# Attention kernel: the loop over heads written out on all engines, and the inverse scales turned beside the third chunk of the first maxima

## The reference, cut to what matters

```python
def reference(x, ctx_2048, ...):          # x (16, 56, 256), ctx (16, 1500, 256)
    x = x + _L0_xattn_ref(_layernorm(x), ctx_2048, Wq, bq, Wkv, bkv, Wp, bp)
    x = x + _L0_ffn_ref(...)              # 32 experts of 96, top 6, and a shared one
    x = x + _L1_xattn_ref(...)            # decayed scan over the context, layernorm
    x = x + _L1_ffn_ref(...)              # 8 experts of 176, top 2
    return x

def _L0_xattn_ref(x, cond, ...):          # 16 heads of 16; 896 queries, 24000 keys, all with all
    q = _fq_sym(q * scale, axis=-1)       # rounded to 127 steps of its own maximum
    k = _fq_sym(k, axis=-1)
    v = _fq_sym(v, axis=2)
    attn = jax.nn.softmax(jnp.einsum('bhqd,bhkd->bhqk', q, k), axis=-1)
    attn = _fq_unsigned(attn, axis=-1)    # rounded to 255 steps of the row's maximum
    out = jnp.einsum('bhqk,bhkd->bhqd', attn, v)
    return out.reshape(B, N, C) @ Wp + bp
```

## Time and profile before

| | us |
|---|---|
| median of 3 runs | 5237.91 |
| runs | 5232.74 to 5238.2 |
| the profiled execution | 5235.59 |
| its span, first to last instruction | 5234.4 |
| busy: PE, DVE, ACT, POOL | 4791.3, 4165.5, 3839.6, 3616.9 |

### The profile page before, as it was taken

The page is one execution under the profiler, slowest core; times in us unless marked ns, Lnnn a source line. Parts: engine busy times, 40 slices in busy tenths (PEclk is TensorE's granted clock), DMA queues, the critical chain, the costliest instruction groups (busy, mean ns, idle before and its releaser), DMA issues. The chain is left out here.

```text
span 5234.4 us, 166575 instructions
## 1 busy us (share of the span) xinstructions
PE 4791.3 (92%) x52761; PEld 1878.9 (36%) x52761; DVE 4165.5 (80%) x6858; ACT 3839.6 (73%) x6406; POOL 3616.9 (69%) x3775
## 2 busy tenths in 40 slices
PE   4888679999999999999999999999999999776979
PEld 2444311333333333333333333333333333224645
DVE  5888679989898988989898989989898988333242
ACT  1444400999998998999899989989999999780101
POOL 1555540888888888888888888888888888991000
PEclk8999855999999999999999999999999999887989
DMA  2555510111111111111111111111111111322000
GB/s 79 181 182 180 166 43 21 31 32 30 34 31 31 31 33 32 29 33 31 33 32 32 33 30 32 32 30 35 30 33 31 32 32 58 123 90 99 34 1 7
DMA packets 221020, 272.99 MB, mean 52 GB/s; under 512 B 34126, under 2 KB 199630, under 8 KB 219387
## 3 DMA queue, kind: packets, MB, share of 16 engines
q1 hardware_dynamic: 169370, 208.24, 14.3%
q10 hardware_dynamic: 50784, 53.76, 3.1%
HBM read 177.31 MB, written 83.10 MB: 50 GB/s over the span
## 5 line engine op out<-in xcount | busy, mean ns | idle before, releaser
L997 ACT ACTIVATE e<-ps_sweep,sk 125x448 f32<-125x448 f32 x6144 | 3503.4, 633 | 281.9 <-ACTq L996 176.2
L1045 DVE TENSOR_REDUCE unit_max<-ps_sweep 128x1 f32<-128x500 f32 x5376 | 3237.1, 670 | 366.7 <-DVEq L1044 345.0
L1180 POOL TENSOR_SCALAR r<-e 125x896 f32<-125x896 f32 x3072 | 2885.0, 956 | 582.7 <-POOLq L1179 263.1
L782 PE MATMUL ps_sweep<-q,k 54*128 54x448 bf16 x5760 | 1860.5, 354 | 9.7 <-PEq L772 3.1
L813 PE MATMUL ps_sweep<-k,q 48*128 48x500 bf16 x5376 | 1748.3, 391 | 60.2 <-PEq L812 53.5
L835 PE MATMUL ps_av<-e,zt 126*17 126x224 f32 x24576 | 1718.3, 355 | 0.0
L828 PE MATMUL ps_av<-r,vt 125*16 125x224 f16 x12288 | 854.3, 268 | 69.7 <-PEq L821 51.6
L813 PEld LDWEIGHTS ps_sweep<-k,q 48*128 48x128 bf16 x5376 | 349.3, 94 | 1253.3 <-issue 1248.0
L782 PEld LDWEIGHTS ps_sweep<-q,k 54*128 54x128 bf16 x5760 | 528.2, 93 | 513.7 <-issue 404.1
L835 PEld LDWEIGHTS ps_av<-e,zt 126*17 126x17 f32 x24576 | 629.3, 96 | 1.4 <-issue 0.2
L828 PEld LDWEIGHTS ps_av<-r,vt 125*16 125x16 f16 x12288 | 302.7, 85 | 777.1 <-issue 776.8
(11 more groups left out here) (207 smaller groups left out, 2264.0 us busy)
## 6 DMA issues: line engine op xcount, KB each, us to landing
k_rows<-krows ACTq DMA_DIRECT2D x48, 1000.0 KB, 6.4
k<-k_rows SPq DMA_DIRECT2D x408, 93.8 KB
k<-k_rows SPq DMA_DIRECT2D x128, 281.2 KB
cx<-in_ctxT SPq DMA_DIRECT2D x48, 500.0 KB, 4.4
v_raw<-kv SPq DMA_DIRECT2D x24, 1000.0 KB
vr<-v_raw SPq DMA_DIRECT2D x128, 187.5 KB
cb<-in_ctxT SPq DMA_DIRECT2D x16, 1500.0 KB, 6.2
gu_w<-in_gu SPq DMA_DIRECT2D x5, 1536.0 KB, 13.7
```

The lines of the kernel that those rows point to most:

```text
L782: pe.matmul(score_bank(i, g, False)[:, 0:HALF], k2[u][:, i * KT:i * KT + P], q2[y][:, g * HALF:(g + 1) * HALF], start=True, stop=True, til ...
L997: act.activation(e[i % SLOTS][0:KT, g, :], score_bank(i, g, both)[0:KT, 0:HALF], ACT.Exp, scale=sk[u][:, i:i + 1]).then_inc(e_wrote, 1)
L1045: top = dve.tensor_reduce(unit_max[:, b, j * NPIECE + at:j * NPIECE + at + 1], ps[:, 0:SB], axis=AX.X, op=ALU.max)
L1180: pool.tensor_scalar(r[i % SLOTS][:, :, :], e[i % SLOTS][0:KT, :, :], 1.0, HALFWORD, ALU.mult, ALU.add)\
```

## The change

Two things. The loops over heads on all five engines are written out: `over_heads` calls `head` for each head with plain numbers, and POOL calls `chunk` 128 times. And on PE the nine groups of transposes, with the wait at the chunk's end, stand in the chunk with j == 2 of head 0, the third, in place of the first.

```diff
-        def over_heads(eng, head):
+        def over_heads(head):
             head(0, None, None, 0, True)
             head(1, 0, None, 1, True)
-            with eng.Fori(0, (HEADS - 4) // 2) as hd:
-                for y in range(2):
-                    head(hd * 2 + 2 + y, hd * 2 + 1 + y, hd * 2 + y, y, True)
-            for y in range(2):
-                head(HEADS - 2 + y, HEADS - 3 + y, HEADS - 4 + y, y, y == 0)
+            for h in range(2, HEADS):
+                head(h, h - 1, h - 2, h % 2, h < HEADS - 1)
             head(None, HEADS - 1, HEADS - 2, 0, False)
...
-                        if not second and head_start and i >= CT - TB * PARTS // 8:
+                        if not second and j == 2 and i >= CT - TB * PARTS // 8:
                             turn_t_rows(i - (CT - TB * PARTS // 8))
-                    if not second and head_start:
+                    if not second and j == 2:
                         pe.wait_ge(t_copied, 3).then_inc(t_copied, -3)
...
-            with pool.Fori(0, HEADS - 1) as h:
-                for j in range(NCH):
-                    chunk(j % 2, h + j // (NCH - 1))
-            for j in range(NCH):
-                chunk(j % 2, HEADS - 1 if j < NCH - 1 else None)
+            for n in range(1, HEADS * NCH + 1):
+                chunk((n - 1) % 2, n // NCH if n < HEADS * NCH else None)
```

More of the change, by code:

```diff
@@ L755, in sp_program @@
             sp.dma_start(sq[:, :, :], q_scale.rearrange("(b p) h -> p b h", p=QB)).then_inc(sq_landed, 16)
-            over_heads(sp, head)
+            over_heads(head)
             store_sums(HEADS - 1)
@@ L962, in pe_program @@
             pe.wait_ge(less_ready, 1).then_inc(less_ready, -1)
-            over_heads(pe, head)
+            over_heads(head)
             for i in (CT - 2, CT - 1):
@@ L1032, in act_program @@
             act.activation(decay[:, :], decay[:, :], ACT.Sigmoid).then_inc(decay_ready, 1)
-            over_heads(act, head)
+            over_heads(head)
             copy_sums()
@@ L1162, in dve_program @@
             dve.wait_ge(sq_landed, 16).then_inc(sq_landed, -16)
-            over_heads(dve, head)
+            over_heads(head)
             dve.wait_ge(bias_landed, 32).then_inc(bias_landed, -32)
```

## The result

| | before | after |
|---|---|---|
| median, us | 5237.23 (4 runs) | 5171.93 (4 runs) |
| runs | 5232.74 to 5238.2 | 5170.57 to 5173.59 |
| profiled execution | 5235.59 | 5173.59 |
| ratio, 95% interval | | 0.9877, 0.986 to 0.9894 |

The change takes 65.3 us off the medians (by the interval of the ratio, 56 to 73) and 62.0 us off the profiled executions. The forecast was 5181 with a range of 5171 to 5194: right in direction and in kind, and 9 us too small a gain. It had 55.5 us for the two parts, so some 6.5 us of the profiled 62.0 need an explanation.

What follows compares the result with a forecast made beforehand. DVE was taken to bound the first head at half clock, PE the heads from about 900 us. Gains of 26.5 + 29 = 55.5 us off 5235.59 gave 5180.1; forecast 5181, range 5171 to 5194.

Steps and rivals of the forecast that it cites:

- Part one: Head 0: moving the turn to the third chunk removes the wait for POOL's scales, 26.5 us, bounds 24.7 to 28.3.
- this stretch moves as it is, about 17.7 us long: Head 0: the turning itself keeps its length at half clock in the new place; only the hole before it goes.
- Rival B: Head 0: the hole reappears elsewhere, at POOL's v_inv or the last copies, so little gain there; 5207 us, chance 0.04.
- Of its bounds: Head 0: gain 28.3 us if waiting pieces hide more, 24.7 if PE refills banks at 0.57 us, hardly above DVE's pace.
- Part two: Twelve looped heads: writing the loops out removes five taken-branch stalls and the half clock behind them, 29 us.
- I give it zero: POOL's loop over heads: its branches cost PE nothing that shows, so writing it out gains 0 us.
- The upper bound of 30.4: Twelve looped heads: the most the written-out loops could gain, taking the straight head's 234.28 us for all twelve.
- 234.3 to 234.8: Heads after the change: every head was to take this many us.
- Rival A: Twelve heads: straight code still stalls at each head's start, so written-out loops bring nothing; 5209 us, chance 0.03.
- Rival C: Written-out code, PE above all: instruction fetching cannot keep up and the kernel gets slower, for instance 5300 us; chance 0.02.
- Rival D: Clock steps around head 1 and the last head fall otherwise, some 3 us each way; forecast including this, chance 0.89.
- The two pages that I had set against each other: Loop branches: one skill page gives about 108 ns (0.5 us gain), the other a fetch stall; the trace sided with the second.

Runs made afterwards that it cites:

- experiment 10: Changed kernel with the nine groups of turns spread over the third and fourth chunks; 5167.73 us, run again 5166.3 beside 5172.04 of the changed kernel.
- Experiment 3: Changed kernel with POOL's loop put back, all other engines straight; 5176.1 us.
- experiment 1: Kernel before with only the turn moved to the third chunk, all loops as before; 5210.13 us.
- experiment 4: Changed kernel with PE's loop alone put back, six passes of two heads with five taken branches; 5197.35 us.
- experiment 5: Changed kernel with the loops of DVE and ACT put back, PE, POOL and SP straight; 5202.08 us.

## Why the prediction was right, and where its size was off

**Part one** held: forecast 26.5 us, measured 26.9 in the window of head 0. The step "this stretch moves as it is, about 17.7 us long" is confirmed by both timelines (727.17 to 744.89 is 17.7). Rival B, the hole appearing elsewhere, is gone: POOL's wait for `v_inv` went from 171.4 to 144.3 us, and head 0 as a whole is shorter by the full length of the hole. Of its bounds one had a wrong reason: I wrote that PE fills a bank in 0.57 us, hardly faster than DVE empties it. 0.57 is the duration of one matmul; the pace of a free PE is 0.43 (experiment 10). That is why the turning could be hidden at all.

**Part two** was right on what the stall is and on where most of the time comes from, and its size was off: 29 us forecast, 34.1 in the twelve heads. (The 1.8 us in heads 1 and 14 say little: head 1 takes 234.1 to 236.6 in the traces of straight kernels.) The term that failed is "I give it zero" for POOL's loop. Experiment 3 has both halves of the sum: with all engines but POOL straight the twelve heads are 28.0 us shorter than before, which is what the 29 were meant for, and POOL's loop is worth 6.1 more. I had looked at one POOL branch and at the waits right behind it. The upper bound of 30.4 came from head 14, in which POOL still had its loop, and for such a kernel it held (28.0). It rested on a single head, though: the 233.99 of the same head in experiment 1 would have made it 33.9. The waits were in the listing by releaser: 57 short waits of PE for `r_ready`, 16.2 us. The 0.4 us by which the loop's first heads were longer than head 14 belong here too, as far as heads can tell: the first heads of the pairs take 234.6 to 234.9 us before, and 233.7 to 234.6 in experiment 4, where PE has its loop and POOL has not. This is also why the heads came out at 233.4 to 234.5 us in the changed kernel where I had written 234.3 to 234.8.

**Rival A**, each head beginning with such a stall even in straight code, did not occur: no wait of PE over 0.8 us in the twelve heads. **Rival C**, slower by fetching, did not either, and its premise was right. The twelve heads have these instruction transfers (packets, MB, share), first in the loop of before, then in the straight code after:

```profile
q8 instruction: 345, 5.65, 0.8%
q14 instruction: 292, 2.39, 0.3%
```

```profile
q8 instruction: 337, 5.52, 0.8%
q14 instruction: 217, 1.78, 0.2%
```

The loop had fetched its body anew at every pass, so writing it out adds no traffic (7.30 MB against 8.04), and the crossings cost nothing that shows. **Rival D** moved the time little: head 1's mean granted clock is 0.99 in both kernels.

The two pages that I had set against each other speak of different parts. The 108 ns that the Trainium skill gives for a compare-and-branch ("Advanced Engine Details and Errata", Control Flow Timing) lie between the 76 ns of the untaken and the 208 ns (median) of the taken branch that PE shows where nothing has to be fetched; the stall comes on top when something has.

## What to carry to other kernels

Look at a loop's end as at any other instruction: find its row, and compare a taken branch with the untaken last one. Write a loop out when the body of an engine is long; a short loop cost next to nothing here. Judge the body engine by engine, since one loop has a different length on each. Do not sum the stops of several engines, and do not call an engine's stop free because that engine has spare time: one look at who waits for it over the whole stretch, not only at the branch, would have shown the missing 6 us as a candidate. And a wait for work that is made late costs its full length when unrelated work stands behind it in the same program; move it to any place behind the producer's end.

## What the runs showed that I had not expected

A stall costs PE more than its length. In the kernel before a branch costs 5.2 us, though it holds PE back about 3.6. Behind it the granted clock is at 0.50 for 3.4 us in which PE is busy throughout (the last row); at half clock that is 1.7 us of work lost, by estimate, and 3.6 and 1.7 are 5.3. In experiment 4 a branch costs 5.7, and there the clock is at 0.50 for longer:

```profile
1581.30:1588.10 6.80, 5.41 (x46) 1.36 (x46) 2.82 (x5) 2.65 (x5) 2.78 (x3) 0.50 0.26 66
```

This also happens when PE has no branch at all but waits for ACT and DVE (experiment 5: 0.83 on the mean over 10 us). A stop of 2 to 3 us on ACT and DVE, with time to spare on both, cost almost as much as one on PE, 5.2 us against 5.7. And a taken branch into a long body held PE about 3.6 us in the attention, where the DMA engines are 13% busy, and 7.1 us in the keys and values stage, where they are 57% busy; that the load is the cause was not tested.
